# A four-layer graph network on one core: the opening in another order, and x of the fourth layer turned by four transposes and copied across by DMA

## The chip, the cores and the metric

One core of a Trainium2 chip runs the whole program. Its engines are TensorE (PE, with its weight loads shown as PEld), VectorE (DVE), ScalarE (ACT), GpSimd (POOL) and SyncE (SP), which here only issues DMAs. The metric is the device time of one execution in microseconds. The kernel before took 1986.62 us in the median of three runs (1986.0 to 1987.79).

## The reference

x has 16 batches of 1024 nodes with 64 features; `adj` is one 1024 x 1024 integer matrix. Four graph layers follow one another, each as `x = layernorm(x + layer(x, adj))`:

- layers 1 and 3, additive attention: `h = x @ W`, `e = leaky_relu(h@a1 + (h@a2).T)`, masked by `adj`, softmax over the neighbours, `elu(attention @ h)`
- layer 2: a softmax for each feature over the neighbours of `softplus(x*w0 + b0)`
- layer 4, attention by dot products, with the node itself always a neighbour:

```python
h = jnp.einsum('bnc,hdc->bhnd', x, Wh)                 # 4 heads
out_h = _gat_layer(h, mask, bh)                        # softmax(h h^T masked) @ h + b, per head
z = leaky_relu(concat(out_h))
h2 = jnp.einsum('bnk,dk->bnd', z, Wo)
out2 = _gat_layer(h2, mask, bo)                        # the same with one head
```
followed by a leaky ReLU, a layer norm with gamma and beta, the residual and the outer layer norm.

## The kernel before

Nodes lie in 8 tiles of 128 partitions; PSUM banks hold 512 columns. Every engine has its own list of work written out by hand, with semaphores between them; a function of a stage is called from the engine's list at a named place, and the order of the calls is the order on that engine.

**The opening** (`opening`). SP issues eight DMAs of 512 KB, one for each row tile of `adj`, then x of batches 1 to 3, small weights, and x of batches 4 to 15 (3 MB). DVE turns each tile to zeros and ones (L407), PE turns it by eight 128 x 128 transposes into one of two PSUM tiles (L451), and ACT (DVE for the last tile) copies it into `keep.mask` (L434, L420). From the row sums a matrix of empty rows is made and turned by eight matmuls (L470), and DVE writes it to `keep.empty` (L425). Among these stands the preparation of batch 0 of the first layer: x is turned (`turn_x`, four transposes, L783), projected (`project`: L791, L800, L806), and the tops of the scores are found and spread (`find_tile_top`, `turn_top`, `find_minus_top`, `find_top`, `spread_tops`, `copy_tops`); `factors` on ACT makes the rows from which the attention weights come.

**The first layer** (`additive_layers`), batch by batch: DVE makes eight tiles of weights (`weigh`, L609) into a ring of four; PE multiplies each with the values (`multiply`, L846, 16 matmuls); `divide` (L616, L619) ends a batch and stands behind the first `weigh` of the next. At the head of a batch PE projects the next batch (`project(n + 1)`) and multiplies the empty rows (`multiply_empty`, L832).

**The fourth layer** (`dot_layer`). A batch has 20 steps: s0 to s7 for the first pair of heads, r0 to r7 for the second, and e0 to e3 for the second attention of the batch before. In each step PE makes two tiles of scores (for s and r twelve matmuls of 512 columns, L1616, L1619, L1622), does a job that stands at this step if there is one, and multiplies the weights of the step before (L1666, eight matmuls; L1681 in e steps); ACT takes the exponent (L1458), DVE masks (L1212). The jobs that concern x of the next batch: POOL copies x into `x_stage`, each tile twice side by side (L1085, at s0); PE turns it at r3 (`turn_x`, eight transposes, L1527), which gives x turned on partitions 0 to 63 and once more on 64 to 127; ACT rounds it to `x_high` (L1401), DVE makes the rest `x_low` (L1166, at r4); PE makes g from them (`make_g`, at e1, L1537 to L1543), DVE multiplies g with `x_high` (`multiply_g`, L1174, at e1); the scores of the next batch begin at its s0. Both copies of x are wanted by the scores, since two heads are multiplied side by side on the two halves of the partitions; `make_g` wants only the half h of the nodes on half h of the partitions. For batch 0 all this stands in the last batch of the third layer, and for batch 1 at r0 to r4 of batch 0.

SP's list in the fourth layer (`sync`): for each batch `spread_recip(b, 0)` (the sums of pair 0 to DRAM, back, inverted by DVE, out and back broadcast), `swap(b - 1)` (half of h copied to the other half of the partitions, high and low part), `store(b - 2)`, `spread_recip(b, 1)`. SP waits in order at each.

## Time and profile before

| | us |
|---|---|
| three runs | 1986.0, 1986.62, 1987.79 |
| the profiled execution, its own time | 1988.66 |
| its span in the trace | 1986.7 |
| PE busy | 1897.6 (96%) |
| DVE busy | 1634.9 (82%) |
| ACT busy | 1246.8 (63%) |
| POOL busy | 581.4 (29%) |

Busy PE is matmul time with modelled ends; the span is from the first instruction to the last. The mean granted TensorE clock was 0.987 of full speed. The opening and the first batches lie at 0 to 60 us, the fourth layer from about 670 us to the end.

### The profile page before, as it was taken

The numbers are of one execution on the slowest core, as the hardware profiler recorded it, in microseconds if no ns is written. First come the engines' busy times: TensorE is split into PE (matmuls) and PEld (weight loads), VectorE is DVE, ScalarE is ACT, GpSimd is POOL, SyncE is SP. The second block draws the span as 40 slices with busy tenths as digits, with TensorE's granted clock in tenths as the row PEclk, the third lists the DMA queues.
The fourth block names the chain that finished last, engine by engine and source line by source line (L and its number), as shares of the span: only waits on it lengthen the run. The fifth ranks groups of instructions, "written<-read, shape, count | busy, mean of one in ns | idle before, by whom it ended". The sixth has DMA issues, their size and how long they took to land.

```text
span 1986.7 us, 51864 instructions
## 1 busy us (share of the span) xinstructions
PE 1897.6 (96%) x22356; PEld 1178.9 (59%) x22356; DVE 1634.9 (82%) x1944; ACT 1246.8 (63%) x2299; POOL 581.4 (29%) x440
## 2 busy tenths in 40 slices
PE   7999899999999899999999999999999999999995
PEld 5888766777888544554545545555455454554554
DVE  5999868878999777878888788888887888878876
ACT  3777776655777676566565665665656656566562
POOL 0333368762433200113122121231221312212124
PEclk9999999998999999999999999999999999999997
DMA  6000000000000001010110100101001011010011
GB/s 177 3 4 3 3 1 1 1 1 3 3 4 3 2 12 33 13 39 3 37 28 12 39 23 18 28 12 39 28 13 38 6 36 28 12 39 23 18 29 33
DMA packets 51947, 42.19 MB, mean 21 GB/s; under 512 B 35208, under 2 KB 38344, under 8 KB 51720
## 3 DMA queue, kind: packets, MB, share of 16 engines
q1 hardware_dynamic: 49816, 38.46, 7.2%
q8 instruction: 176, 2.88, 0.6%
q10 hardware_dynamic: 1904, 0.43, 0.1%
q14 instruction: 51, 0.42, 0.1%
HBM read 25.76 MB, written 4.72 MB: 15 GB/s over the span
## 4 chain that ended last, share of the span: by engine, by line
PE 60%; DVE 5%; issue 1%; DMA 0%; ACT 0%; SPq 0%; POOL 0%; ACTq 0%; DVEq 0%; POOLq 0%
PE fourth_ps_out L1666 22%; PE fourth_ps_scores L1616 8%; PE fourth_ps_out L1681 6%; PE fourth_ps_scores L1619 5%; PE fourth_ps_scores L1622 5%; DVE fourth_weights L1212 3%; PE fourth_ps_scores L1640 2%; PE fourth_ps_prep L1558 2%; PE fourth_ps_scores L1649 1%; PE fourth_ps_scores L1643 1%; PE fourth_ps_scores L1646 1%; PE fourth_ps_prep L1568 1%; PE fourth_ps_prep L1550 1%; PE fourth_ps_prep L1527 1%; DVE fourth_cat L1191 1%
## 5 line engine op out<-in xcount | busy, mean ns | idle before, releaser
L1212 DVE TENSOR_TENSOR fourth_weights<-fourth_weights,keep_mask 128x1024 f32<-128x1024 f32 x512 | 666.0, 1342 | 109.2 <-ACT fourth_weights L1458 107.2
L1458 ACT ACTIVATE fourth_weights<-fourth_ps_scores 128x1024 f32<-128x1024 f32 x512 | 497.0, 1024 | 347.3 <-PE fourth_ps_scores L1622 326.0
L1666 PE MATMUL fourth_ps_out<-fourth_weights,fourth_x_stage 128*64 128x512 f32 x2048 | 498.2, 605 | 4.9 <-DVE fourth_weights L1212 4.9
L609 DVE SCALAR_TENSOR_TENSOR additive_weights<-additive_ps_row,additive_gain,keep_mask 128x1024 f32<-128x1024 f32 x256 | 319.4, 1267 | 2.7 <-ACT additive_ps_row L724 2.7
L846 PE MATMUL additive_ps_out<-additive_values,additive_weights 128*64 128x65 f32 x8192 | 285.7, 226 | 28.3 <-DVE additive_weights L609 23.5
L846 PEld LDWEIGHTS additive_ps_out<-additive_values,additive_weights 128*64 128x64 f32 x8192 | 258.9, 140 | 53.5 <-DVE additive_weights L609 36.2
L1666 PEld LDWEIGHTS fourth_ps_out<-fourth_weights,fourth_x_stage 128*64 128x64 f32 x2048 | 124.2, 136 | 251.6 <-issue 216.2
L1616 PE MATMUL fourth_ps_scores<-fourth_g_high,fourth_x_high 64*128 64x512 f32 x1024 | 229.5, 445 | 2.1 <-ACT fourth_weights L1458 2.1
L1616 PEld LDWEIGHTS fourth_ps_scores<-fourth_g_high,fourth_x_high 64*128 64x128 f32 x1024 | 95.8, 183 | 200.6 <-issue 102.2
L1619 PE MATMUL fourth_ps_scores<-fourth_g_high,fourth_x_low 64*128 64x512 f32 x1024 | 202.0, 390 | 0.0
L1622 PE MATMUL fourth_ps_scores<-fourth_g_low,fourth_x_high 64*128 64x512 f32 x1024 | 201.6, 389 | 0.0
L1465 ACT ACTIVATE fourth_weights<-fourth_ps_scores 128x1024 f32<-128x1024 f32 x128 | 125.6, 1026 | 113.5 <-PE fourth_ps_scores L1649 109.7
L1219 DVE TENSOR_TENSOR fourth_weights<-fourth_weights,keep_mask 128x1024 f32<-128x1024 f32 x128 | 153.0, 1236 | 41.6 <-ACT fourth_weights L1465 41.6
L1090 POOL TENSOR_TENSOR fourth_biased<-fourth_mixed,keep_rows_in 128x512 f32<-128x512 f32 x15 | 32.0, 2135 | 439.2 <-DVE fourth_mixed L1227 439.2
L1681 PEld LDWEIGHTS fourth_ps_out<-fourth_h_values,fourth_weights 128*64 128x64 f32 x4096 | 124.6, 138 | 29.6 <-issue 29.0
L1681 PE MATMUL fourth_ps_out<-fourth_h_values,fourth_weights 128*64 128x65 f32 x4096 | 133.3, 223 | 0.5 <-DVE fourth_weights L1219 0.5
L1622 PEld LDWEIGHTS fourth_ps_scores<-fourth_g_low,fourth_x_high 64*128 64x128 f32 x1024 | 96.4, 184 | 22.7
L1619 PEld LDWEIGHTS fourth_ps_scores<-fourth_g_high,fourth_x_low 64*128 64x128 f32 x1024 | 96.6, 185 | 11.1
L176 POOL TENSOR_TENSOR additive_norm_rstd<-additive_norm_variances,keep_minus_half 128x8 f32<-128x8 f32 x32 | 53.5, 1670 | 162.2 <-DVE additive_norm_variances L170 162.2
L185 ACT ACTIVATE keep_x<-additive_norm_y,additive_norm_offset,additive_norm_rstd 128x64 f32<-128x64 f32 x256 | 88.0, 429 | 7.4 <-POOL additive_norm_offset L179 7.4
L165 ACT ACTIVATE additive_norm_squares<-additive_norm_y,additive_norm_minus_mean 128x64 f32<-128x64 f32 x256 | 85.2, 340 | 2.5 <-DVE additive_norm_minus_mean L159 2.5
L545 POOL TENSOR_TENSOR additive_values<-additive_hidden,additive_values 128x512 f32<-128x512 f32 x32 | 33.8, 1057 | 155.1 <-ACT additive_values L721 155.1
(243 smaller groups left out, 2762.6 us busy)
## 6 DMA issues: line engine op xcount, KB each, us to landing
fourth_recip_wide<-recip_out SPq DMA_DIRECT2D x128, 128.0 KB, 3.0
opening_adj<-in_adj SPq DMA_DIRECT2D x8, 512.0 KB, 8.2
fourth_h_high<-fourth_h_high SPq DMA_DIRECT2D x32, 128.0 KB, 2.8
fourth_h_low<-fourth_h_low SPq DMA_DIRECT2D x32, 128.0 KB, 2.4
out<-keep_x SPq DMA_DIRECT2D x15, 256.0 KB, 2.6
dens_out<-fourth_mixture SPq DMA_DIRECT2D x64, 4.0 KB
keep_x<-in_x SPq DMA_DIRECT2D x1, 768.0 KB, 13.4
fourth_dens<-dens_out SPq DMA_DIRECT2D x32, 8.0 KB, 1.6
```

Of the source, the lines that this page charges most:

```text
L185: act.activation(x[:, t, :], self.y[n % 2][:, t, :], ACT.Identity, bias=self.offset[:, t:t + 1], scale=self.rstd[:, t:t + 1]).then_inc(x_w ...
L609: dve.scalar_tensor_tensor(out=weights[t % RING][:, :], in0=ps_row[s][:, :], scalar=gain[s][:, t:t + 1], in1=keep.mask[:, t, :].bitcast(F3 ...
L846: last = pe.matmul(ps_out[part, i * WIDE:i * WIDE + AUG], weights[t % RING][:, i * P + c * SIDE:i * P + (c + 1) * SIDE], values[s][:, t, 0 ...
L1212: dve.tensor_tensor(buf, buf, keep.mask[:, st.t, cols(half)].bitcast(F32).unsqueeze(1) .to_broadcast([P, 2, HALF]), ALU.mult).then_inc(wei ...
L1219: dve.tensor_tensor(buf[:, :], buf[:, :], keep.mask[:, 2 * p + u, :].bitcast(F32), ALU.mult)\
L1458: act.activation(weights[st.slot + half][:, :], ps_scores[half][:, :], ACT.Exp)\
L1465: act.activation(weights[slot + u][:, :], ps_scores[u][:, :], ACT.Exp).then_inc(exp_ready, 2)
L1616: pe.matmul(ps_scores[half][:, cols(g)], x_high[s][rows(g), nodes], g_high[pair][rows(g), cols(half)], start=True, stop=False)
L1619: pe.matmul(ps_scores[half][:, cols(g)], x_low[s][rows(g), nodes], g_high[pair][rows(g), cols(half)], start=False, stop=False)
L1622: last = pe.matmul(ps_scores[half][:, cols(g)], x_high[s][rows(g), nodes], g_low[pair][rows(g), cols(half)], start=False, stop=True)
L1666: last = pe.matmul(ps_out[rows(g), cols(half)], x_stage[st.s][:, st.t, g, :], weights[st.slot + half][:, cols(g)], start=(st.t == 0), stop ...
L1681: last = pe.matmul(ps_out[c * SIDE:(c + 1) * SIDE, i * WIDE:i * WIDE + AUG], weights[slot + u][:, i * P + c * SIDE:i * P + (c + 1) * SIDE] ...
```

## The change

Two things are changed.

**The opening's order.** On PE x of batch 0 is turned after mask tile 1 (before: 4), projected after tile 3 (5), its top turned after tile 4 and spread after tile 5 (both after tile 7), x of batch 1 turned after tile 6 (after the tops); batch 1 is projected at the end of the opening's list, ahead of `multiply_empty(0)`, as before, but the call stands in another function. What waited for `empty_ready` (written behind the last read of the PSUM tile that holds the empty rows) in front of batch 1's row matmuls now waits for `last_copied`; the two PSUM tiles `turned0` and `turned1` change places for that, and `first_w` moves to other columns of `ps_x`. On ACT the copies of x, hidden and mean move up among the mask copies; on DVE `copy_w`, `copy_products` and the tops move.

**x of the fourth layer.** `x_stage` holds tile t and tile t + 4 side by side, once each; four transposes then give half h of the nodes on half h of the partitions. ACT and DVE round and lower each half on its 64 partitions. SP copies each half to the other half of the partitions, four DMAs of 128 KB for each batch (`fill_x`); `multiply_g` and the first scores wait for them. In SP's list `fill_x(b + 1)` stands between `swap(b - 1)` and `store(b - 2)`, and those of batches 0 and 1 at its head.

```diff
@@ -339,3 +339,3 @@
     mem.psum("beside1")
-    turned = [mem.psum(f"turned{k}") for k in range(2)]
+    turned = [mem.psum(f"turned{k}") for k in range(2)][::-1]
     degree = mem.sbuf("degree", [P, TILES])
...
@@ -347,3 +347,3 @@
     adj_v = ins["adj"].rearrange("(t p) j -> p t j", p=P)
-    first_w, first_products = additive.ps_x[0:DIM, 0:DIM], additive.ps_row[0][:, 0:P + 1]
+    first_w, first_products = additive.ps_x[0:DIM, HALF:HALF + DIM], additive.ps_row[0][:, 0:P + 1]
 
...
@@ -408,6 +408,10 @@
                               accum_out=degree[:, t:t + 1]).then_inc(masked, 1)
-            if t == 1:
+            if t == 2:
                 weights.copy_w(0, first_w)
-            if t == 3:
+            if t == 4:
                 weights.copy_products(0, first_products)
+            if t == 6:
+                additive.find_tile_top(0)
+        additive.find_minus_top(0)
+        additive.find_top(0)
         dve.wait_ge(masked, TILES)
...
@@ -415,5 +419,3 @@
                           ALU.is_equal).then_inc(empty_ready, 1)
-        additive.find_tile_top(0)
-        additive.find_minus_top(0)
-        additive.find_top(0)
+        additive.copy_tops(0)
         dve.wait_ge(turned_full, TILES)
...
@@ -421,3 +423,2 @@
                         turned[1][:, :].rearrange("j (t i) -> j t i", i=P)).then_inc(last_copied, 1)
-        additive.copy_tops(0)
         dve.wait_ge(consts, 13)
...
@@ -436,8 +437,10 @@
                .then_inc(copied, 1)
-            if i == 4:
+            if i == 1:
                 additive.copy_x(0)
-        additive.copy_hidden(0)
-        additive.copy_mean(0)
+            if i == 3:
+                additive.copy_hidden(0)
+                additive.copy_mean(0)
+            if i == 5:
+                additive.copy_x(1)
         additive.factors(0, 0)
-        additive.copy_x(1)
 
...
@@ -455,13 +458,15 @@
                 weights.turn_w(0, first_w)
+                pe.wait_ge(keep.first_x_loaded, 16)
+                additive.turn_x(0)
             if i == 2:
                 weights.multiply_w(0, first_products)
-            if i == 4:
-                pe.wait_ge(keep.first_x_loaded, 16)
+            if i == 3:
                 pe.wait_ge(weights.prod_ready, 2)
-                additive.turn_x(0)
-            if i == 5:
                 additive.project(0)
-        additive.turn_top(0)
-        additive.spread_tops(0)
-        additive.turn_x(1)
+            if i == 4:
+                additive.turn_top(0)
+            if i == 5:
+                additive.spread_tops(0)
+            if i == 6:
+                additive.turn_x(1)
         pe.wait_ge(copied, TILES - 1)
...
@@ -472,2 +477,3 @@
         last.then_inc(empty_full, 1)
+        additive.project(1)
 
...
@@ -475,3 +481,3 @@
     stage.sync, stage.gpsimd, stage.vector, stage.scalar, stage.tensor = sync, gpsimd, vector, scalar, tensor
-    stage.empty_ready = empty_ready
+    stage.empty_ready, stage.last_copied = empty_ready, last_copied
     return stage
...
@@ -857,3 +863,4 @@
             ahead = b + 1 < BATCH
-            if ahead:
+            if ahead and n:
+
                 project(n + 1)
...
@@ -918,3 +925,3 @@
     h_norm = sb("h_norm", [P, HALF], F32R)
-    x_stage = [sb(f"x_stage{k}", [P, TILES, 2, DIM]) for k in range(2)]
+    x_stage = [sb(f"x_stage{k}", [P, PER_BANK, HALVES, DIM]) for k in range(2)]
     x_high = [sb(f"x_high{k}", [P, NODES], F32R) for k in range(2)]
...
@@ -1028,2 +1036,10 @@
 
+    def fill_x(b, s):
+
+        for parts, ready, filled in ((x_high[s], x_high_ready, x_high_filled), (x_low[s], x_low_ready, x_low_filled)):
+            sp.wait_ge(ready, 2 * (b + 1))
+            for h in range(HALVES):
+                sp.dma_start(parts[rows(1 - h), cols(h)].bitcast(F32), parts[rows(h), cols(h)].bitcast(F32))\
+                  .then_inc(filled, 16)
+
     def spread_recip(b, pair):
...
@@ -1063,2 +1079,4 @@
     def sync():
+        fill_x(0, 0)
+        fill_x(1, 1)
         for b in range(BATCH):
...
@@ -1067,2 +1085,4 @@
                 swap(b - 1)
+            if b and b + 1 < BATCH:
+                fill_x(b + 1, 1 - b % 2)
             if b > 1:
...
@@ -1084,4 +1104,5 @@
         wait(pool, weights_used, used)
-        pool.tensor_copy(x_stage[s][:, :, :, 1:DIM], keep.x[:, b, :, 1:DIM].unsqueeze(2)
-                         .to_broadcast([P, TILES, 2, DIM - 1])).then_inc(staged, 1)
+
+        pool.tensor_copy(x_stage[s][:, :, :, 1:DIM],
+                         keep.x[:, b, :, 1:DIM].rearrange("p (h t) d -> p t h d", h=HALVES)).then_inc(staged, 1)
 
...
@@ -1163,6 +1184,6 @@
     def lower_x(b, s):
+        dve.wait_ge(x_high_ready, 2 * b + 2)
         for h in range(HALVES):
-            dve.wait_ge(x_high_ready, 2 * b + h + 1)
-            dve.tensor_tensor(x_low[s][:, cols(h)], ps_prep[:, cols(h)], x_high[s][:, cols(h)].bitcast(F32),
-                              ALU.subtract).then_inc(x_low_ready, 1)
+            dve.tensor_tensor(x_low[s][rows(h), cols(h)], ps_prep[rows(h), cols(0)],
+                              x_high[s][rows(h), cols(h)].bitcast(F32), ALU.subtract).then_inc(x_low_ready, 1)
 
...
@@ -1172,2 +1193,3 @@
         dve.wait_ge(g_full, n + 1)
+        dve.wait_ge(x_high_filled, 32 * (b + 1))
         wait(dve, norm_full, n)
...
@@ -1398,5 +1420,5 @@
     def round_x(b, s):
+        act.wait_ge(x_full, b + 1)
         for h in range(HALVES):
-            act.wait_ge(x_full, 2 * b + h + 1)
-            act.activation(x_high[s][:, cols(h)], ps_prep[:, cols(h)], ACT.Copy).then_inc(x_high_ready, 1)
+            act.activation(x_high[s][rows(h), cols(h)], ps_prep[rows(h), cols(0)], ACT.Copy).then_inc(x_high_ready, 1)
 
...
@@ -1525,7 +1547,6 @@
         pe.wait_ge(staged, b + 1)
-        for t in range(TILES):
-            last = pe.transpose(ps_prep[:, chunk(t)], x_stage[s][:, t, :, :].rearrange("p k c -> p (k c)"),
+        for t in range(PER_BANK):
+            last = pe.transpose(ps_prep[:, chunk(t)], x_stage[s][:, t, :, :].rearrange("p h c -> p (h c)"),
                                 keep.ident[:, :])
-            if t % PER_BANK == PER_BANK - 1:
-                last.then_inc(x_full, 1)
+        last.then_inc(x_full, 1)
 
...
@@ -1611,2 +1632,4 @@
             pe.wait_ge(x_low_ready, 2 * (st.b + 1))
+            pe.wait_ge(x_high_filled, 32 * (st.b + 1))
+            pe.wait_ge(x_low_filled, 32 * (st.b + 1))
         pair, s, nodes = st.phase, st.s, chunk(st.t)
...
@@ -1665,3 +1688,3 @@
             for g in range(2):
-                last = pe.matmul(ps_out[rows(g), cols(half)], x_stage[st.s][:, st.t, g, :],
+                last = pe.matmul(ps_out[rows(g), cols(half)], x_stage[st.s][:, st.t % PER_BANK, st.t // PER_BANK, :],
                                  weights[st.slot + half][:, cols(g)], start=(st.t == 0),
...
@@ -2520,3 +2543,3 @@
             if n == 1:
-                nc.tensor.wait_ge(start.empty_ready, 2)
+                nc.tensor.wait_ge(start.last_copied, 1)
             if n == BATCH:
```

PE in the opening, kernel before, from the transposes of mask tile 3 to the turning of batch 1's x (`turned` are the PSUM tiles of the mask and of the empty rows, `ps_x` and `ps_row` hold the projections):

```order
L451 MATMUL opening_turned1<-keep_ident,opening_rows 128x128 x8
L451 MATMUL opening_turned0<-keep_ident,opening_rows 128x128 x8
L783 MATMUL additive_ps_x<-keep_ident,keep_x 128x128 x4
L451 MATMUL opening_turned1<-keep_ident,opening_rows 128x128 x8
L791 MATMUL additive_ps_x<-keep_w_aug0,additive_x_sum0 128x64
L800 MATMUL additive_ps_x<-keep_w_aug0,additive_x_turned 128x65 x8
L806 MATMUL additive_ps_row0<-additive_x_turned,keep_w_wide0 128x512 x2
L451 MATMUL opening_turned0<-keep_ident,opening_rows 128x128 x8
L451 MATMUL opening_turned1<-keep_ident,opening_rows 128x128 x8
L813 MATMUL additive_ps_x<-keep_ident,additive_tile_top 1x128
L818 MATMUL additive_ps_x<-additive_top_pair,keep_ones 128x2
L783 MATMUL additive_ps_x<-keep_ident,keep_x 128x128 x4
```

The same place now, from mask tile 3 to the empty rows:

```order
L454 MATMUL opening_turned0<-keep_ident,opening_rows 128x128 x8
L797 MATMUL additive_ps_x<-keep_w_aug0,additive_x_sum0 128x64
L806 MATMUL additive_ps_x<-keep_w_aug0,additive_x_turned 128x65 x8
L812 MATMUL additive_ps_row0<-additive_x_turned,keep_w_wide0 128x512 x2
L454 MATMUL opening_turned1<-keep_ident,opening_rows 128x128 x8
L819 MATMUL additive_ps_x<-keep_ident,additive_tile_top 1x128
L454 MATMUL opening_turned0<-keep_ident,opening_rows 128x128 x8
L824 MATMUL additive_ps_x<-additive_top_pair,keep_ones 128x2
L454 MATMUL opening_turned1<-keep_ident,opening_rows 128x128 x8
L789 MATMUL additive_ps_x<-keep_ident,keep_x 128x128 x4
L454 MATMUL opening_turned0<-keep_ident,opening_rows 128x128 x8
L475 MATMUL opening_turned1<-keep_ident,opening_empty_wide 128x128 x8
```

The turning of x has gone up past tiles 2 to 4 and stands above this piece; the projection has gone up past tiles 4 and 5, the tops and batch 1's x past tile 7, so that only the empty rows stand behind tile 7. The projection of batch 1 follows them in both kernels.

DVE in the opening, kernel before, from mask tile 4 to the first attention weights (L407 masks a tile, L414 writes the empty rows, L420 copies the last mask tile):

```order
L407 TENSOR_SCALAR opening_rows,opening_degree<-opening_adj 128x1024 x4
L414 TENSOR_SCALAR opening_empty_wide<-opening_degree 128x1024
L586 TENSOR_REDUCE additive_tile_top<-additive_hidden 128x1
L591 TENSOR_REDUCE additive_top_pair<-additive_ps_x 1x1
L596 TENSOR_SCALAR additive_top_pair<-additive_top_pair 1x1
L420 CAST keep_mask<-opening_turned1 128x8x128
L601 COPY additive_tops<-additive_ps_x 128x2
L425 TENSOR_SCALAR keep_empty<-opening_turned0,opening_row_used 128x1024
L609 SCALAR_TENSOR_TENSOR additive_weights0<-additive_ps_row0,additive_gain0,keep_mask 128x1024
```

The same place now, from mask tiles 5 and 6:

```order
L407 TENSOR_SCALAR opening_rows,opening_degree<-opening_adj 128x1024 x2
L592 TENSOR_REDUCE additive_tile_top<-additive_hidden 128x1
L407 TENSOR_SCALAR opening_rows,opening_degree<-opening_adj 128x1024
L597 TENSOR_REDUCE additive_top_pair<-additive_ps_x 1x1
L602 TENSOR_SCALAR additive_top_pair<-additive_top_pair 1x1
L418 TENSOR_SCALAR opening_empty_wide<-opening_degree 128x1024
L607 COPY additive_tops<-additive_ps_x 128x2
L422 CAST keep_mask<-opening_turned0 128x8x128
L426 TENSOR_SCALAR keep_empty<-opening_turned1,opening_row_used 128x1024
L615 SCALAR_TENSOR_TENSOR additive_weights0<-additive_ps_row0,additive_gain0,keep_mask 128x1024
```

The top of the tiles (`tile_top`), which waits for ACT's copy of the projection, now stands in front of the last mask tile, and the other tops in front of the empty rows and the last mask copy.

SP in the fourth layer, kernel before, batch 2's part (`x_high1` and `x_low1` are the buffers of batch 3):

```order
L1034 DMA dens_out<-fourth_mixture0 1x1024 x2
L1037 DMA fourth_dens<-dens_out 128x16
L1040 DMA recip_out<-fourth_head_recip 128x16
L1046 DMA fourth_recip_wide0<-recip_out 64x512 x4
L1022 DMA fourth_h_high<-fourth_h_high 64x512 x2
L1026 DMA fourth_h_low<-fourth_h_low 64x512 x2
L1052 DMA out<-keep_x 128x8x64
L1034 DMA dens_out<-fourth_mixture1 1x1024 x2
```

The same place now:

```order
L1050 DMA dens_out<-fourth_mixture0 1x1024 x2
L1053 DMA fourth_dens<-dens_out 128x16
L1056 DMA recip_out<-fourth_head_recip 128x16
L1062 DMA fourth_recip_wide0<-recip_out 64x512 x4
L1030 DMA fourth_h_high<-fourth_h_high 64x512 x2
L1034 DMA fourth_h_low<-fourth_h_low 64x512 x2
L1042 DMA fourth_x_high1<-fourth_x_high1 64x512 x2
L1042 DMA fourth_x_low1<-fourth_x_low1 64x512 x2
L1068 DMA out<-keep_x 128x8x64
L1050 DMA dens_out<-fourth_mixture1 1x1024 x2
```

Two rows of two DMAs each are new, in front of the store and of the sums of pair 1.

## Rows read from the trace of the kernel before

**Rows 1.** The page, section 4: the chain that ended last, by engine.

```profile
PE 60%; DVE 5%; issue 1%; DMA 0%; ACT 0%; SPq 0%; POOL 0%; ACTq 0%; DVEq 0%; POOLq 0%
```

**Rows 2.** Windows: stretch, its length; busy PE, PEld, DVE, ACT, POOL; clock, DMA.

```profile
1236.76:1317.44 80.68, 80.33 (x697) 42.19 (x695) 67.14 (x65) 49.28 (x58) 19.02 (x11) 1.00 0.09 25
```

**Rows 3.** Timeline of PE, fourth layer: start, us, instruction (steps r2, r3).

```profile
1255.90 0.66 PE L1599 MATMUL fourth_ps_prep<-keep_ident,fourth_h_plain 128*128 128x128 f32 x4
...
1259.95 1.09 PE L1527 MATMUL fourth_ps_prep<-keep_ident,fourth_x_stage 128*128 128x128 f32 x8
```

**Rows 4.** Timeline of PE, step s2; then waits of 860 to 1900 us.

```profile
1225.58 1.08 PE L1666 MATMUL fourth_ps_out<-fourth_weights,fourth_x_stage 128*64 128x512 f32 x4 [0.35 <-DVE fourth_weights L1212]
...
PE fourth_ps_out L1666 <- DVE fourth_weights L1212: 4.3, 12, 0.4
```

**Rows 5.** Timelines of POOL and DVE there; L1085 by source; DVE in batch 15.

```profile
1222.37 2.07 POOL L1085 COPY fourth_x_stage<-keep_x 128x1008 f32<-128x1008 f32 x1
...
1223.47 2.05 DVE L1212 TENSOR_TENSOR fourth_weights<-fourth_weights,keep_mask 128x1024 f32<-128x1024 f32 x1
...
L1085 POOL COPY fourth_x_stage<-keep_x x16: 1021/2072/2073, 649.3 to 1787.2; 128x1008 f32<-128x1008 f32 x16
...
1867.91 4.69 DVE L1212 TENSOR_TENSOR fourth_weights<-fourth_weights,keep_mask 128x1024 f32<-128x1024 f32 x4
```

**Rows 6.** SP's issues, their landing (L1022), and DVE, steps r4 to e1.

```profile
1268.24 1.24 SPq L1026 DMA_DIRECT2D fourth_h_low<-fourth_h_low  x2
...
DMA to landing us min/median/max: 2.5/2.8/3.8
...
1284.46 1.22 DVE L1174 TENSOR_TENSOR fourth_products<-fourth_ps_prep,fourth_x_high 128x1024 fp32r<-128x1024 f32 x1 [2.07 <-PE fourth_ps_prep L1543]
```

**Rows 7.** Timelines of ACT and DVE, batch 0 of the fourth layer.

```profile
704.96 1.08 ACT L1401 ACTIVATE fourth_x_high<-fourth_ps_prep 128x512 fp32r<-128x512 f32 x2
...
710.23 1.23 DVE L1174 TENSOR_TENSOR fourth_products<-fourth_ps_prep,fourth_x_high 128x1024 fp32r<-128x1024 f32 x1 [0.80 <-PE fourth_ps_prep L1543]
```

**Rows 8.** Timeline of PE in the opening.

```profile
5.99 1.94 PE L451 MATMUL opening_turned<-keep_ident,opening_rows 128*128 128x128 f32 x8 [5.99 <-DVE opening_rows L407]
...
10.56 0.31 PE L210 MATMUL additive_ps_x<-keep_ident,keep_w 64*64 64x64 f32 x1 [0.28 <-DMA keep_a_cols<-in_L_gnn_a]
...
14.45 0.80 PE L224 MATMUL additive_ps_row<-weights_a_wide,weights_w_turned 64*128 64x129 f32 x2
...
18.79 1.04 PE L451 MATMUL opening_turned<-keep_ident,opening_rows 128*128 128x128 f32 x8
...
20.20 0.43 PE L791 MATMUL additive_ps_x<-keep_w_aug,additive_x_sum 128*128 128x64 f32 x2 [0.38 <-ACT additive_x_turned L688]
20.57 1.11 PE L800 MATMUL additive_ps_x<-keep_w_aug,additive_x_turned 64*128 64x65 f32 x16
21.51 1.08 PE L806 MATMUL additive_ps_row<-additive_x_turned,keep_w_wide 64*128 64x512 f32 x4
...
25.43 0.38 PE L813 MATMUL additive_ps_x<-keep_ident,additive_tile_top 128*1 128x128 f32 x2 [0.94 <-DVE additive_tile_top L586]
...
27.16 1.95 PE L470 MATMUL opening_turned<-keep_ident,opening_empty_wide 128*128 128x128 f32 x16
```

**Rows 9.** Timeline of DVE, opening to the end of batch 0.

```profile
29.23 1.28 DVE L425 TENSOR_SCALAR keep_empty<-opening_turned,opening_row_used 128x1024 fp32r<-128x1024 f32 x1 [1.73 <-PE opening_turned L470]
...
30.43 2.47 DVE L609 SCALAR_TENSOR_TENSOR additive_weights<-additive_ps_row,additive_gain,keep_mask 128x1024 f32<-128x1024 f32 x2
...
46.46 0.21 DVE L616 RECIPROCAL additive_recip<-additive_ps_out 128x8 f32<-128x8 f32 x1 [1.82 <-PE additive_ps_out L846]
```

**Rows 10.** Timeline of PE in batch 0; window 33 to 34 us.

```profile
35.15 1.15 PE L846 MATMUL additive_ps_out<-additive_values,additive_weights 128*64 128x65 f32 x32
...
43.52 1.15 PE L846 MATMUL additive_ps_out<-additive_values,additive_weights 128*64 128x65 f32 x32 [1.66 <-issue]
...
33.00:34.00 1.00, 1.00 (x4) 0.00 (x0) 0.98 (x2) 0.10 (x1) 0.00 (x0) 0.50 1.04 215
```

5 lines of the change are left out of this document (3 added, 2 removed).

## The prediction

> **What bounds the kernel now.** I read the page first, then the fourth layer batch by batch, then the opening. The chain that ended last is on PE for 60% of the span and hardly anywhere else [rows 1]; the reader is to see that what leaves PE's own list is worth its full time as long as nothing else takes its place. The window over one batch of the fourth layer shows how far that holds: PE is busy for 80.33 of 80.68 us, DVE for 67.1, ACT for 49.3 [rows 2]. Only 0.35 us of a batch are idle on PE, and the timeline names them: one wait at step s2, for DVE's masked weights; 12 of them in the stretch of 860 to 1900 us, 4.3 us together [rows 4]. The opening is another matter: there PE, ACT and DVE wait for each other, the first attention weights of batch 0 start at 30.43 us, and batch 0 ends, by the division, at 46.46 [rows 9]. From there on the first layer runs at its own pace, so what that division gains is the gain of the whole opening.
>
> **The change part by part.** *Four transposes fewer on PE.* Eight transposes of staged x take 1.09 us, four transposes of the same shape (h, one step earlier) 0.66 [rows 3]. Both rows carry the same tail of the last matmul, so four fewer save 0.43 us. PE has no gap around them, so this is on the path, 15 times in the fourth layer (batches 1 to 15): 6.5 us. For batch 0 they stand in the third layer's last batch, where ACT waits for them; I count 0.43 there too. Sum 6.9, bounds 6.0 and 7.0.
>
> *POOL's copy halved.* The copy of 1008 elements took 1.02 us at its shortest and 2.07 in the median [rows 5]. At s1 it starts at 1222.37, at the same moment as a mask multiplication of DVE, and ends at 1224.44; the next multiplication of DVE, begun at 1223.47, takes 2.05 us, where an undisturbed one takes half of 2.36 or so: in batch 15, which has no copy, four take 4.69 us, 1.17 each [rows 5]. So the two take turns, and DVE pays some 0.85 us for the copy. Those are the weights for which PE waits 0.35 us at 1225.58 [rows 4], and the wait is missing in batch 15. With 504 elements the copy's own turn is half, 0.5 us, and DVE is free about 0.5 us earlier: more than 0.35, so the wait should go, with 0.15 to spare. 13 batches (2 to 14) have both copy and wait: 13 x 0.35 = 4.6 us. Bounds: 0, if DVE is held as long as before or the stall is only shifted, and 4.9.
>
> The Trainium skill's page "SBUF — State Buffer", section "Who interferes with whom", gives the mechanism: a DVE instruction with two SBUF inputs and a GpSimd instruction that reads SBUF exclude each other for the whole instruction, whichever comes first. By that rule the hold is the copy's own length, and the trace agrees (2.05 against 1.17 us).
>
> *ACT and DVE on 64 partitions.* Two roundings and two subtractions of 512 columns remain, each on half the partitions. Two roundings take 1.08 us [rows 7], over 512 columns each; nothing here shows half the partitions to be faster, and neither engine is on the path at r3 or r4. I take nothing; bounds 0 and 0.
>
> *Four DMAs for each batch.* SP issues two transfers of 128 KB in 1.24 us, and such a transfer lands 2.5 to 3.8 us after its issue [rows 6]. In SP's list the new ones come after the swap of h, whose last pair is issued at 1268.24 to 1269.48. So they are issued until about 1272, and land by 1275.5. The first reader, `multiply_g` on DVE, starts at 1284.46 [rows 6], 9 us later, and behind it stand the masks of step e1, for which PE would wait. The store and the sums of pair 1 behind them in SP's queue come later than 1272 anyway. Cost 0, and the cover is 9 us. The tight place is batch 0, where x of batch 1 is rounded until 706.04 and multiplied at 710.23 [rows 7]: two issues of 0.6 us and a landing of 2.8 make 709.6, by the slowest landing 710.5. That is 0 to 0.3 us, once. Transfers on disjoint halves of the partitions are advised against in the skill ("DMA: Bandwidth & Descriptors", "Rules for kernel authors": they serialize); even four after each other, 4 x 2.8 = 11 us from 1269.5, end before 1284.46 here.
>
> *The opening, first part: when the first weights can start.* The last things ahead of them are tile 7, the empty rows on PE and their copy on DVE. PE's new list is now nearly without gaps, so I add it up from the weights' arrival at 10.56 [rows 8]: turning W 0.31, x 0.66 [rows 3], tile 2 1.94, the products 0.80, tile 3 1.94; this makes 16.2. Then the projection 0.43 + 1.11 + 1.08 and four tiles of 1.04 (the fast rate, which before was reached by 18.79), two small matmuls for the tops of 0.38, x of batch 1 0.66: 24.4. The empty rows 1.95, and DVE's copy 1.28 [rows 9]: 27.6, against 30.43. ACT's copies run beside it, the last one perhaps 0.2 late: 27.8. Gain 2.6; bounds 1.5 and 4. (That DVE now waits for the projection before the last tile costs nothing as long as PE is the later one.)
>
> *The opening, second part: batch 0.* Before, DVE had its weights ready from 31.7, but PE multiplied the first only at 35.15 [rows 10], since the projection of batch 1 waited for x, turned late. In that stretch PE's granted clock was 0.50, i.e. 1.2 instead of 2.4 GHz, after half-idle microseconds (33 to 34 in rows 10). Now x of batch 1 is ready during the opening; its projection follows the empty rows at 26.4 and is over by 29, when the first weights come. Batch 0 then goes at DVE's pace: nine multiplications of 1.2 (two take 2.47, rows 9) and 0.7 of small ones, 11.5 us to the division, where before it took 46.46 - 30.43 = 16.0. So the division could stand at 27.8 + 11.5 = 39.3, 7.2 us earlier. One piece of the old delay I keep: at 41.9 PE stopped for 1.66 us, for nothing that the profile shows, in the middle of one tile's products [rows 10], while the 3 MB of x were still landing. Those come at the same time as before, and PE now runs more instructions beside them. With 1.7 off I take 5.5 for the whole opening; bounds 2.6 (all of the second part is eaten up) and 7.5.
>
> The skill ("Runtime: NRT & Kernel Launch", "Instruction fetch mechanics") says that instructions stream in by blocks over the engine's own DMA queue, mostly hidden. The gap of 1.66 us is not hidden; if it is the fetch, by that page's claim it would be an exception, and without it the opening would gain 7.2.
>
> **The sum.** 5.5 + 6.9 + 4.6 = 17.0 us. Against the profiled execution's own 1988.66 (span 1986.7) this gives 1971.7; that execution is 2.0 above the median of 1986.62, so the median after is 1969.6.
>
> **The rivals.** (1) *The wait at s2 stays.* For it: the copy has a four-deep access pattern now and POOL's spans are rough; 0.15 us to spare is little. Against: batch 15. It gives 1986.6 - 12.4 = 1974.2. (2) *The opening gains only its first part.* For it: the unexplained 1.66 us under the load; the division can't come before PE has finished, and each stop like that counts nearly in full. Against: DVE, not PE, sets the pace afterwards. 2.6 + 6.9 + 4.6 = 14.1: 1972.5. Both together 1977.1. (3) *All of it and the gap too*: 7.2 + 6.9 + 4.6: 1967.9. (4) *Slower.* One mechanism: `multiply_g` waits in each batch for the two high copies, and holds the masks behind it. The two are issued at 1269.5 and 1270.1 and cost nothing until one lands later than 1284.46, some 14 us after its issue, against 3.8 at most seen [rows 6]; to end at slower by 0.2% (4 us) it must eat the 17 as well, 21 us over 14 batches, 1.5 us each, a landing of 16 us. It would give 1990.6. Only SP arriving late at `fill_x` could do it, if the sums of pair 0 ran that late; they don't [rows 6]. (5) *The change doesn't do what it says*: PE's saved time turns up as waiting for ACT's exponents. Against it, ACT is idle for 31 us of a batch and DVE for 13 [rows 2]. It would leave the opening and the wait: 1976.5.
>
> **How the numbers follow.** Forecast (every term near its middle) 52%; rival 1 14%; rival 2 14%, both together 4%; rival 3 9%; rival 5 4%; slower 2%; about no change 1%. The range from 1966 to 1976.5 takes in the first five but the doubled one and half of rival 5. A measurement of this kernel can tell 0.2%, 4 us, from no change. Faster by over 0.2%: 97%; within: 1%; slower: 2%.
>
> **What would show it.** In the changed kernel's trace: the division of batch 0 near 41 us; the first weights near 27.8 and the first products by 30; four transposes of staged x in a 0.66 row; no wait of PE at s2 and the mask multiplication beside the copy near 1.6 us; the period of a batch 80.68 - 0.78 = 79.9 us; the new copies issued near r4 and landing before e0. A period of 80.25 would mean that the wait has stayed, one of 80.68 that the transposes were covered, one above that new waits came in. The forecast is wrong if the period is off by more than 0.3 us or the division of batch 0 stands outside 39 to 44 us.

## The result and the profile after

The changed kernel takes 1972.62 us in the median of four runs (1971.68 to 1975.19), beside 1987.18 us for the kernel before on the same chip: a ratio of 0.9929, 95% interval 0.9918 to 0.9941. The gain is 14.6 us; 17.0 were forecast, and the time is 3.0 us over the predicted 1969.6, inside the range. The kernel before was timed anew beside every run below, with medians from 1987.18 to 1988.95 us, so ratios compare two runs better than their medians do.

The profiled execution had a time of its own of 1975.19 us and a span of 1973.1, 13.6 us less than the 1986.7 of before. Three marks cut both spans into stages: the division of batch 0 (the opening's end), and the first and the last product over x in the fourth layer. All marks are starts of instructions. The profiled execution is the slowest of the four, 2.6 us above their median.

| stage | before | after | gain | forecast |
|---|---|---|---|---|
| start to the division of batch 0 | 46.46 | 42.68 | 3.8 | 5.5 |
| from there to the first product over x | 627.5 | 626.3 | 1.1 | 0.43 |
| first to last product over x (s, r, e steps) | 1251.1 | 1239.2 | 11.9 | 11.05 |
| last product over x to the end | 61.7 | 64.9 | -3.2 | 0 |

So the two middle rows came out a little better than forecast, the first gained less, and the last stage became longer, which no term of the sum had.

*Opening.* Timeline of DVE in the changed kernel (start, duration, instruction, in brackets the idle time before it), answering to [rows 9]:

```profile
25.37 1.28 DVE L426 TENSOR_SCALAR keep_empty<-opening_turned,opening_row_used 128x1024 fp32r<-128x1024 f32 x1 [1.73 <-PE opening_turned L475]
26.57 2.47 DVE L615 SCALAR_TENSOR_TENSOR additive_weights<-additive_ps_row,additive_gain,keep_mask 128x1024 f32<-128x1024 f32 x2
...
42.68 0.21 DVE L622 RECIPROCAL additive_recip<-additive_ps_out 128x8 f32<-128x8 f32 x1 [4.80 <-PE additive_ps_out L852]
```

The first weights start at 26.57, against 30.43 before and 27.8 in the forecast. The division waits 4.80 us for PE. The timeline of PE says why, beside [rows 8, 10], and the windows below it (stretch, length, busy PE, PEld, DVE, ACT, POOL with counts, granted clock, DMA share, GB/s) show what came with it:

```profile
14.02 1.24 PE L454 MATMUL opening_turned<-keep_ident,opening_rows 128*128 128x128 f32 x8
...
27.99 1.15 PE L852 MATMUL additive_ps_out<-additive_values,additive_weights 128*64 128x65 f32 x32
...
32.53 2.25 PE L852 MATMUL additive_ps_out<-additive_values,additive_weights 128*64 128x65 f32 x69
38.17 4.48 PE L852 MATMUL additive_ps_out<-additive_values,additive_weights 128*64 128x65 f32 x91 [3.38 <-issue]
```

```profile
36.00:38.00 2.00, 0.00 (x0) 0.00 (x0) 1.88 (x2) 0.00 (x0) 0.00 (x0) 1.00 1.08 221
38.00:40.00 2.00, 1.83 (x34) 1.83 (x36) 0.00 (x0) 0.00 (x0) 0.00 (x0) 0.56 1.12 219
40.00:42.00 2.00, 2.00 (x48) 2.00 (x46) 0.00 (x0) 0.00 (x0) 0.00 (x0) 0.58 0.94 187
```

The reader is to see three things. The projection of batch 1 and the first products came as planned, by 30. Then PE stopped for 3.38 us behind its 165th product, the same place where it had stopped for 1.66 us before. And after the stop the granted clock was 0.56 to 0.58, close to the lower of its two levels (0.50, 1.2 GHz), so that the last 91 products took 4.48 us. Before, at a granted clock of 1.00, they took 2.90:

```profile
43.52 2.90 PE L846 MATMUL additive_ps_out<-additive_values,additive_weights 128*64 128x65 f32 x91 [1.66 <-issue]
```

From the first weights to the division it was 16.0 us before (30.43 to 46.46) and 16.1 after (26.57 to 42.68). So the whole gain of the opening, 3.8 us, lies ahead of the first weights, and the second part of the forecast (11.5 us for this stretch, and 1.7 for the stop) brought nothing.

*Fourth layer.* One batch, by windows [rows 2]; the four transposes [rows 3]; POOL's copy and DVE's multiplications beside it [rows 5]; SP's issues [rows 6]:

```profile
1206.59:1286.44 79.85, 79.85 (x697) 41.69 (x689) 66.94 (x64) 49.39 (x58) 18.58 (x11) 1.00 0.13 33
...
1249.49 0.66 PE L1549 MATMUL fourth_ps_prep<-keep_ident,fourth_x_stage 128*128 128x128 f32 x4
...
1212.37 1.65 POOL L1106 COPY fourth_x_stage<-keep_x 128x504 f32<-128x504 f32 x1
...
1212.34 5.03 DVE L1234 TENSOR_TENSOR fourth_weights<-fourth_weights,keep_mask 128x1024 f32<-128x1024 f32 x4
...
1257.80 1.24 SPq L1034 DMA_DIRECT2D fourth_h_low<-fourth_h_low  x2
1259.08 1.24 SPq L1042 DMA_DIRECT2D fourth_x_high<-fourth_x_high  x2
1260.36 1.24 SPq L1042 DMA_DIRECT2D fourth_x_low<-fourth_x_low  x2
...
1273.61 1.23 DVE L1196 TENSOR_TENSOR fourth_products<-fourth_ps_prep,fourth_x_high 128x1024 fp32r<-128x1024 f32 x1 [2.10 <-PE fourth_ps_prep L1564]
```

PE is busy for the whole 79.85 us; the period was forecast as 79.9. The wait of [rows 4] is gone in every batch but the first. The four multiplications beside the copy take 5.03 us, where four with no copy took 4.69 [rows 5]; the one that the copy holds takes 1.63 us, as forecast (near 1.6), instead of 2.05. `multiply_g` (L1196) starts 13.3 us after both high DMAs were issued and waits for PE, not for a DMA.

*The end.* PE's waits in each kernel, the changed one first (engine, what it waits to write, for whom; us in total, times, longest):

```profile
PE fourth_ps_scores L1610 <- DVE fourth_cat L1267: 4.5, 1, 4.5
```

```profile
PE fourth_ps_scores L1589 <- DVE fourth_cat L1245: 2.7, 1, 2.7
```

DVE in turn waited there for the reciprocals of the last heads, sent to memory and spread from there; after, then before:

```profile
1926.62 0.69 DVE L1264 TENSOR_TENSOR fourth_cat<-fourth_ps_prep,fourth_sloped 128x512 f32<-128x512 f32 x1 [2.70 <-DMA fourth_recip_wide<-recip_out]
```

```profile
1941.70 0.69 DVE L1242 TENSOR_TENSOR fourth_cat<-fourth_ps_prep,fourth_sloped 128x512 f32<-128x512 f32 x1 [0.95 <-DMA fourth_recip_wide<-recip_out]
```

The DMA views of the 4 us around that small write of 8 KB (issued at 1917.74 after, 1934.56 before) show a packet of the queue q8, which carries PE's instructions, in one and none in the other. After:

```profile
q1 hardware_dynamic: 144, 0.01, 2.3%
q8 instruction: 1, 0.02, 1.6%
...
recip_out<-fourth_head_recip SPq DMA_DIRECT2D x1, 8.0 KB, 3.1
```

Before:

```profile
q1 hardware_dynamic: 280, 0.24, 21.9%
...
recip_out<-fourth_head_recip SPq DMA_DIRECT2D x1, 8.0 KB, 1.4
```

(The larger count of q1 before is the spreading of the reciprocals, which begins sooner behind the early landing.) After, the write lands after 3.1 us instead of 1.4. Narrower windows show what held it. The write is 128 packets of 64 bytes and 16 of 4 bytes, 144 in all. Changed kernel, 1918.4 to 1919.2 us, then 1919.6 to 1920.0; nothing moves between them:

```profile
q1 hardware_dynamic: 135, 0.01, 10.9%
q8 instruction: 1, 0.02, 8.0%
...
q1 hardware_dynamic: 9, 0.00, 1.5%
```

The packet of instructions starts 0.93 us after the write's issue and takes 1.02; the last 9 packets of the write (one sixteenth of 144, so probably the share of one of the 16 DMA engines) move only when it is over, at 2.0 us. Before, all 144 had moved in the microsecond from 1935 to 1936. The late landing made 1.7 us; PE then waited 4.5 us, its clock fell (0.50 from 1930 to 1934 us; the second half of the output projection took 1.97 us instead of 1.08), and 3.2 us were lost in all.

### The profile page after: what moved, and what is told of

It reads as the page before. It is cut to its first block, busy times and chain, and to the rows that moved or that the text cites. A ratio compares the mean times of both kernels' runs of the same rounds, so it can differ in the third digit from the quotient of the medians.

```text
span 1973.1 us, 51833 instructions
## 1 busy us (share of the span) xinstructions
PE 1888.3 (96%) x22292; PEld 1169.6 (59%) x22292; DVE 1632.1 (83%) x1944; ACT 1248.5 (63%) x2299; POOL 574.9 (29%) x440
## 4 chain that ended last, share of the span: by engine, by line
PE 64%; DVE 1%; DMA 0%; ACT 0%; issue 0%; POOL 0%; SPq 0%; ACTq 0%; DVEq 0%; POOLq 0%
PE fourth_ps_out L1689 24%; PE fourth_ps_scores L1639 9%; PE fourth_ps_out L1704 6%; PE fourth_ps_scores L1642 6%; PE fourth_ps_scores L1645 6%; PE fourth_ps_scores L1663 2%; PE fourth_ps_prep L1579 2%; PE fourth_ps_scores L1666 2%; PE fourth_ps_scores L1672 1%; PE fourth_ps_scores L1669 1%; PE fourth_ps_prep L1589 1%; PE fourth_ps_prep L1571 1%; PE fourth_ps_prep L1620 0%; PE fourth_ps_prep L1549 0%; PE fourth_ps_prep L1564 0%; PE fourth_ps_prep L1561 0%
## 5 line engine op out<-in xcount | busy, mean ns | idle before, releaser
L852 PE MATMUL additive_ps_out<-additive_values,additive_weights 128*64 128x65 f32 x8192 | 286.3, 227 | 30.9 <-DVE additive_weights L615 24.3
L852 PEld LDWEIGHTS additive_ps_out<-additive_values,additive_weights 128*64 128x64 f32 x8192 | 259.6, 140 | 56.0 <-DVE additive_weights L615 37.2
L1642 PEld LDWEIGHTS fourth_ps_scores<-fourth_g_high,fourth_x_low 64*128 64x128 f32 x1024 | 96.5, 185 | 11.2
```

Of the source, the lines that this page charges most:

```text
L852: last = pe.matmul(ps_out[part, i * WIDE:i * WIDE + AUG], weights[t % RING][:, i * P + c * SIDE:i * P + (c + 1) * SIDE], values[s][:, t, 0 ...
L1642: pe.matmul(ps_scores[half][:, cols(g)], x_low[s][rows(g), nodes], g_high[pair][rows(g), cols(half)], start=False, stop=False)
```

## The experiments

Two theories for the stop of PE in batch 0. **Load theory:** PE's own instructions come in blocks through the DMA engines, and a block is late while the 3 MB of x fill them. **Place theory:** the stop belongs to its place in PE's list. For the rest: each term of the sum by itself.

### The halves of the change: open_only, turn_only

`open_only` has the changed code up to the first layers and the fourth layer of before; `turn_only` the reverse.

> The opening's new order alone; x is turned by eight transposes as before. If the two halves of the change are independent: first weights of batch 0 near 26.6 us, division of batch 0 at 42.7 as in the changed kernel (PE stopped for about 3.4 us in batch 0), period of a fourth-layer batch 80.7 with the wait at s2, total about 4 to 5 us under the kernel before: 1982.5. Rival: the opening's gain is eaten up by the second layer, then within 1 us of the kernel before.

> The turning of x alone (four transposes, halved copy on POOL, DMAs for the rest); the opening is the old one. Forecast from the prediction's terms: 6.9 + 4.6 = 11.5 us under the kernel before, 1975.7; period 79.86; division of batch 0 at 46.5 with the stop of 1.7 us. With open_only the two gains should add up to the whole (14.6 measured); a sum over 17 would mean that the parts disturb each other.

Measured: open_only 1982.92 us, ratio 0.9973 [0.9963, 0.9983]; turn_only 1978.07, 0.9950 [0.9935, 0.9965]; the kernel before beside them 1987.85. The gains are 4.9 and 9.8, 14.7 together, beside 14.6 for the whole: they add up, as far as intervals of 2 to 3 us to either side can tell. turn_only stays 1.7 short of its forecast; its trace has the full 12.0 between the first and the last product over x, and the late write at the end as well (3.6 us to landing, 64.1 us from the last product to the end).

### The load: load_late, load_parts, load_split, before_parts

```
# load_late: one line ahead of the 3 MB load
+ sp.wait_ge(additive.mixed_ready, 2)
# load_parts (and before_parts, the same on the kernel before)
- sp.dma_start(keep.x[:, 4:BATCH, :, :], x_rows(ins)[:, 4:BATCH, :, :]).then_inc(keep.x_loaded[1], 16)
+ for b in range(4, BATCH):
+     sp.wait_ge(additive.mixed_ready, 2 * (b - 3))
+     if b > 4:
+         sp.wait_ge(keep.x_loaded[1], 16 * (b - 4))
+     sp.dma_start(keep.x[:, b, :, :], x_rows(ins)[:, b, :, :]).then_inc(keep.x_loaded[1], 16)
# load_split: the loop with its dma_start alone, no waits
# in load_parts, before_parts and load_split PE's waits for x_loaded[1] count the twelve loads
```

> The changed kernel, with the 3 MB of x (batches 4 to 15) issued only after batch 0 has been divided. Theory (PE's own instruction stream waits behind the load): no stop of PE in batch 0, the division near 39 us instead of 42.7, but a stop of 1 to 4 us in batch 1 or 2, between 40 and 60 us, while the load runs then; total 1970 to 1973. Rival (the stop belongs to the place in PE's list): the stop of about 3.4 us stays at the 165th product of batch 0, division at 42.7, total 1972.6.

> The changed kernel, with the 3 MB of x in twelve loads of 256 KB, one after each division of batches 0 to 11. Theory (instructions wait behind the load): stops of at most about 1 us, division of batch 0 near 39 us, what follows 4 us earlier, total near 1968.6. Rival (the place in the list): the stop stays, 1972.6. Rival (each small load stops PE for about 1 us): twelve small stops, total above 1975.

> The changed kernel with the 3 MB of x cut into twelve loads of 256 KB as in load_parts, but issued one behind the other at the old place, with no pause between them. Theory (a block of instructions waits as long as the queues of the DMA engines are full, whatever the loads' size): the stop in batch 0 stays, 3 us or so, total 1972.6. Rival (a single large load is the trouble): stop under 1 us, division of batch 0 near 38 us, total near 1968.

> The kernel before, with x loaded in twelve pieces, one after each division, and nothing else changed. Theory (the stop of 1.66 us at the 165th product is the load's doing): no stop, division of batch 0 at about 44.8 instead of 46.5, total 1.7 us less, 1985.5. Rival (the place in the list): stop and time unchanged, 1987.2. It also gives what the opening's order is worth where no load stands in its way: division here against load_parts' 37.8 us, about 7.

Measured: load_late 1976.82, 0.9943 [0.9928, 0.9958]; load_parts 1967.83, 0.9901 [0.9885, 0.9918]; load_split 1965.38, 0.9884 [0.9869, 0.9898]; before_parts 1985.54, 0.9987 [0.9977, 0.9997].

In load_late the stop moved with the load. Timeline of PE, batch 1, and the window there:

```profile
51.80 1.03 PE L853 MATMUL additive_ps_out<-additive_values,additive_weights 128*64 128x65 f32 x27 [2.73 <-issue]
```

```profile
50.00:60.00 10.00, 8.20 (x114) 6.31 (x115) 3.52 (x6) 2.10 (x6) 1.86 (x2) 0.66 0.41 86
```

Batch 0 was divided at 36.67 there, 6 us earlier than in the changed kernel, but the third division stands at 69.27 against 69.17: all was given back. The place theory has fallen. The total of 1976.82 is above the expected 1970 to 1973. It is 4.2 over the changed kernel's by the medians, 2.8 by the ratios, whose intervals overlap, and 1.3 by the spans of the two traces; the rest stays open.

The traces also tie each stop to a block of instructions. In all nine profiles with a stop, PE goes on 2.7 to 2.9 us after a packet of q8 has started: 35.41 and 38.17 in the changed kernel, 40.84 and 43.52 before, 39.87 and 42.62 in turn_only, 49.05 and 51.80 in load_late. And the place is a fixed one in PE's list. Counted with weight loads and semaphore instructions, 705 instructions lie ahead of the stop in all eight profiles that stop in batch 0. In load_late it is 1473, which is 768 more, exactly three blocks of 256.

In load_parts and load_split there is no stop, and the divisions stand at 37.82 and 37.10. In load_parts 256 KB moved once in each batch; its total is within 0.8 us of the expected 1968.6. load_split was a miss of the load theory as I had put it: the queues were not empty, and I had expected the stop. What differs is how long a block of instructions waits. The DMA views of 26 to 34 us, first of the changed kernel, then of load_split, by queue (packets, MB, share of 16 engines):

```profile
q1 hardware_dynamic: 1445, 1.45, 85.2%
...
keep_x<-in_x SPq DMA_DIRECT2D x1, 0.2 KB, 17.6
```

```profile
q1 hardware_dynamic: 6543, 1.65, 110.3%
q8 instruction: 1, 0.02, 1.0%
...
keep_x<-in_x SPq DMA_DIRECT2D x8, 256.0 KB, 4.9
```

With the single load no block of instructions moved in these 8 us; the next came at 35.4, and PE went on at 38.17. In load_parts, where no load runs then, it came at 30.2. In load_split, whose twelve issues take SP 14.04 us, it came at 30.9, although the engines were as busy as in the changed kernel (1.65 MB in these 8 us against 1.45). So the cause is that the load is one DMA, and not the bytes that move. What it is about the one DMA, no run separates. Two things differ: all of it is handed over at once and lands 17.6 us after the issue, a small load after 4.9; and its packets are of 1 KB (1445 packets for 1.45 MB), those of the small loads of 256 bytes (6543 for 1.65 MB). The twelve are also handed over no faster than they move: an issue takes SP 1.17 us there, and 0.37 in load_parts. A single load with packets of 256 bytes was not run. Where the block waits, the traces don't show either. The Trainium skill ("Runtime: NRT & Kernel Launch", "Instruction fetch mechanics") says that instructions are fetched in blocks of 16 KiB, 256 instructions, mostly hidden. The changed kernel's page agrees on the block: section 3 has, for PE's 22,292 matmuls and as many weight loads,

```profile
q8 instruction: 176, 2.88, 0.6%
```

which is 253 instructions to a packet of 16 KB, and 256 with PE's 549 semaphore instructions. But the crossing was not hidden at this place: it cost 1.66 us before and 3.38 after.

before_parts gives the fourth corner. Division of batch 0, means over the profiled executions (in brackets how many, and the lowest and highest):

| | one load of 3 MB at the old place | load later, or in twelve pieces |
|---|---|---|
| old order of the opening | 46.0 (2: 45.56, 46.46) | 43.59 (1) |
| new order | 42.1 (6: 41.15 to 42.86) | 37.2 (5: 36.63 to 37.89) |

The last cell holds load_late, load_parts, combined, load_split and split_sooner. The new order is worth 3.9 us under the load and 6.4 without it; the load costs the old order 2.4 us and the new one 4.9. The first weights themselves start anywhere from 25.13 to 26.75 us with the new order, so the stretch from them to the division tells more: 11.4 us in each of these five, beside the 11.5 of the sum, and 16.1 in the changed kernel; in the old order 14.3 without the load and 16.0 under it. before_parts had no stop and gained 1.9 us, as expected (1.7), but its division came 1.2 us before the expected 44.8.

### The wait at s2 and the transposes: long_copy, turned_twice

```
# long_copy: the stage holds everything twice, the second set is not read
- x_stage = [sb(f"x_stage{k}", [P, PER_BANK, HALVES, DIM]) for k in range(2)]
+ x_stage = [sb(f"x_stage{k}", [P, 2, PER_BANK, HALVES, DIM]) for k in range(2)]
...
+     .unsqueeze(1).to_broadcast([P, 2, PER_BANK, HALVES, DIM - 1])).then_inc(staged, 1)
# turned_twice
- for t in range(PER_BANK):
+ for t in [*range(PER_BANK)] * 2:
```

> The changed kernel with POOL's copy of staged x made as long as before (1008 elements, each value written twice; the second set is not read), four transposes and the DMAs kept. Theory (DVE is held for the length of the copy): the mask multiplication beside it takes about 2.05 us again, PE waits 0.35 us at s2 in 13 batches, period 80.25 instead of 79.86, total 4.6 us over the changed kernel, 1977.2. Rival (the wait went because the copy's pattern or the list around it changed): period 79.86, 1972.6.

> The changed kernel with its four transposes of staged x done twice over, into the same place (eight in all). Theory (each four are on the path with 0.43 us): period 79.86 + 0.43 = 80.29 with no wait at s2; 6.9 us in all over the changed kernel, 1979.5. It also adds 128 instructions to PE's list (64 matmuls and their weight loads), half a block of its instruction stream at the end: if it is such a block that delayed the last reciprocals, they may land early here (1.4 us after their issue instead of 3.1), and the end is 2 to 3 us shorter: 1977. Rival (the transposes are covered by waiting for DVE): period 79.86, 1972.6.

Measured: long_copy 1978.61, 0.9955 [0.9941, 0.9970]; turned_twice 1979.20, 0.9952 [0.9936, 0.9969]. Timelines of POOL, DVE and PE in long_copy, then its waits:

```profile
1213.27 2.07 POOL L1106 COPY fourth_x_stage<-keep_x 128x1008 f32<-128x1008 f32 x1
...
1213.23 5.46 DVE L1235 TENSOR_TENSOR fourth_weights<-fourth_weights,keep_mask 128x1024 f32<-128x1024 f32 x4
...
1216.47 1.08 PE L1690 MATMUL fourth_ps_out<-fourth_weights,fourth_x_stage 128*64 128x512 f32 x4 [0.35 <-DVE fourth_weights L1235]
...
PE fourth_ps_out L1690 <- DVE fourth_weights L1235: 4.8, 14, 0.4
```

The longer copy alone brings the wait back, in the same place and size; the period is 80.25 (1213.27 to 1293.52), and the stretch between first and last product over x grows from 1239.2 to 1244.5, 5.3 us. In turned_twice the period is 80.23 and that stretch 1245.1: four transposes more cost 5.9 us in 14 or 15 batches, about 0.41 each. The two together explain 11.2 of the 11.9 us; the other 0.7 stay open. In the medians both came out slower than expected: long_copy by 1.4 us (1977.2), turned_twice by 2.2 (1977 with an early landing at the end).

turned_twice tested the end as well, and there the expectation held: its write of the last reciprocals landed in 1.4 us. With the half block of added instructions, the packet of q8 nearest to the write starts 1.7 us before its issue and is over before any of the write moves:

```profile
recip_out<-fourth_head_recip SPq DMA_DIRECT2D x1, 8.0 KB, 1.4
```

From the last product over x to the end it took 62.1 us. In the profiles that keep the last inversion at e2 this stretch goes with that one landing: where SP waited 1.42 or 1.43 us for it (before, open_only, before_parts, turned_twice, load_split) it is 60.6 to 62.1 us long; where SP waited 3.1 to 3.6 us (the changed kernel, turn_only, load_late, long_copy, fills_twice) 63.6 to 65.1, and in each of these five a packet of instructions moves in the stretch of the landing. load_parts lies between, with 2.5 and 61.9 us. The length of PE's list alone doesn't decide it: load_split has the changed kernel's list, and its packet starts 1.66 us after the issue, when the write has landed. Tenths of a microsecond do: in turn_only the packet starts at 1.60 us, and yet 9 packets of the write come behind it, at 2.5. Why they hadn't moved with the other 135, at 0.75 to 1.1 us, stays open.

### The DMAs: fills_twice

```
+ wait(sp, again_filled, 64 * b)
+ for parts, again in ((x_high[s], again_high), (x_low[s], again_low)):
+     for h in range(HALVES):
+         sp.dma_start(again[rows(1 - h), :], parts[rows(h), cols(h)].bitcast(F32)).then_inc(again_filled, 16)
```

> The changed kernel with each batch's four fills of x issued a second time, behind the first four, into memory that nobody reads; SP issues eight DMAs of 128 KB where there were four. Theory (a cover of 9 us and more, nothing waits for SP here): period 79.86, total within 1 us of the changed kernel, 1972.6. Rival (SP's queue is nearly on the path: the store and the sums of pair 1 stand behind them): period above 80.5, total above 1982.

Measured: 1973.35, 0.9925 [0.9910, 0.9940], beside the changed kernel's 0.9929. The period is 79.83. The DMAs cost nothing, nor would twice as many. In the changed kernel they are issued 0.6 us apart and land 2.2 to 3.7 us after their issues, so the 11 us that the prediction allowed for them one after the other were not needed.

### The end, and a better kernel: recip_sooner, combined, split_sooner

```
- if at == "e2":
+ if at == ("e1" if st.last else "e2"):
      invert_heads(b, 1)
```

> The changed kernel; in the last batch alone, DVE inverts the sums of heads 2 and 3 one step sooner (before the masks of e2 instead of behind them). Theory (at the end of the x heads the program waits for the reciprocals' way through memory, 1.0 us where no block of instructions is in its way and 2.7 to 3.3 where one is): no wait of DVE for the spread reciprocals, PE's wait ahead of the second output projection under 2 us instead of 4.5, PE's clock does not fall there; total 1 to 3 us under the changed kernel, near 1970.5. Rival (that wait was hidden by others): no change, 1972.6.

> The changed kernel with both: x in twelve loads and the last reciprocals one step sooner. Expected: the gain of load_parts (4.8) and that of recip_sooner, which has little left over where the reciprocals came early anyway: 1966.5, between 1965.5 and 1968. Rival: the shorter program puts a wait elsewhere at the end, 1968 or more.

> load_split and recip_sooner together: x in twelve loads one behind the other, and the last reciprocals one step sooner. Expected: no stop in batch 0, the division near 37 us, no wait of DVE for the spread reciprocals whatever block of instructions comes by, so the end after the last product over x of 60.5 to 62 us. Since load_split's own last reciprocals came early (1.4 us after their issue), little is left: 1964.5 to 1966, against load_split's 1965.4. Rival (load_split's gain was one lucky place of the blocks of instructions): the stop or the late reciprocals come back, 1968 or more.

Measured: recip_sooner 1971.86, 0.9920 [0.9904, 0.9936]; combined (with load_parts) 1966.89, 0.9895 [0.9879, 0.9912]; split_sooner (with load_split) 1967.67, 0.9895 [0.9878, 0.9911]. The mechanism works in the trace, if not in full (PE still waits 2.5 us, where under 2 were expected): in recip_sooner DVE waits for ACT, no more for the DMA,

```profile
1925.06 0.69 DVE L1264 TENSOR_TENSOR fourth_cat<-fourth_ps_prep,fourth_sloped 128x512 f32<-128x512 f32 x1 [0.70 <-ACT fourth_sloped L1528]
...
PE fourth_ps_scores L1610 <- DVE fourth_cat L1267: 2.5, 1, 2.5
```

and the end takes 61.9 us instead of 64.9 (61.5 and 61.4 in the other two). But in the times it is not told apart: 0.8 us under the changed kernel, with overlapping intervals. A loss of 3 us at the end may thus belong to the profiled execution and not to every one; the others have no trace. Where the write landed early anyway it brings nothing, as split_sooner shows beside load_split: it was expected at 1964.5 to 1966 and came 1.7 us above that, close to its rival's 1968. combined met its 1966.5. The best median of all is load_split, 1965.38, 7 us under the changed kernel (9 by the ratios) and with an interval clear of it; load_parts, combined and split_sooner have intervals that overlap with it.

## Why the prediction was right, and where it was off

The forecast held: faster, 1972.62 in a range of 1966 to 1976.5. The fourth layer came by the mechanism that was named. The opening's figure came in part by luck, since two errors of opposite sign lie in it, and the total lies on rival 2's 1972.5 only because a loss at the end, which was in no sum, met small gains elsewhere. By its steps:

- *Four transposes fewer*, 6.9: right. The row of 0.66 stands there, and four more cost 5.9 (turned_twice; the term has 6.45 for that stretch). Rival 5 (the time turns up as waiting) is refuted: PE is busy for all 79.85 us of a batch.
- *POOL's copy halved*, 4.6: right in cause and size. The wait is gone, and the longer copy alone brings it back (long_copy, 5.3 us). Rival 1 (the wait stays) is refuted. The Trainium skill's page "SBUF — State Buffer", section "Who interferes with whom", by which the hold would be the copy's own length, is borne out in the difference: DVE's four multiplications take 0.43 us more (5.46 against 5.03) when the copy is 0.42 us longer (2.07 against 1.65). Half the elements are not half the copy, though: at its shortest it took 1.02 us with 1008 elements and 0.60 with 504, where the forecast had 0.5. So the multiplication beside it became 0.42 us shorter (2.05 to 1.63), of which 0.35 were needed.
- *64 partitions and four DMAs*, 0: right (fills_twice); rival 4 had nothing to start from. The tight place of batch 0 is mis-added in the prediction: 706.04, two issues of 0.6 and a landing of 2.8 make 710.0, not 709.6. It didn't matter, for no `multiply_g` waits for a DMA, in batch 0 neither.
- *The opening, first part*, 2.6: too low, it gained 3.9. PE's rows were at the fast rate sooner than in [rows 8]: tile 3 took 1.24 us at 14.02, where I had added 1.94. The sum also adds the projection's three rows at full length, 2.6 us, but they overlap: the next row starts 2.2 us after the first of them. PE then waited 0.82 us for ACT's copy of the mask, more than the 0.2 that were allowed.
- *The opening, second part*: the step that failed is "One piece of the old delay I keep". The term of 1.66 us was mis-sized. Without the single load the division stands at 37.2, earlier than the 39.3 of the sum only because the first weights are; the 11.5 us behind them are right (11.4). Under the load it stands at 42.1, since the old 1.66 became a stop of 3.2 to 3.4 us plus 1.6 us or more for the lower clock after it: 4.7 us from the first weights on, where the sum had 1.7. (The row 33 to 34 of [rows 10], which the prediction calls half idle, has PE busy throughout; it shows the clock of 0.50, the idle time lies before it.) PE comes to its 165th product 7 us sooner, in the middle of the load instead of at its end, while the block of instructions is held back by 5 us in either place (35.4 instead of 30.2 us; in the old order 40.8 instead of the 35.7 of before_parts). The whole opening gained 3.8 in the pair of profiles, 3.9 by the means, for 5.5. Rival 2 named this mechanism, and it is what happened: the opening gained its first part alone. Only that part was larger than its 2.6. The sign for the forecast being wrong, a division outside 39 to 44 us, was too wide to show this.
- *The end*, not in the sum: 3.2 us lost in the profiled execution. Nothing that the change does is near it. The list of PE became shorter by 96 instructions, so the places where its blocks are fetched moved, and one of them fell on a small DMA that others wait for. I had asked of every added DMA what it collides with, and not of PE's instructions.

In the sum: 17.0 forecast, less 1.7 in the opening and 3.2 at the end, plus 0.9 in the fourth layer and 0.7 between, the last without a known cause, make the 13.6 of the spans.

## What to carry to other kernels

A gap of PE that "waits for nothing" during a large load is worth an experiment before any work on the order around it: here twelve loads for one (load_split) brought 7 us, half of what the whole change had brought. To see whether it is the instruction stream, look for a packet of the instruction queue shortly before the engine goes on. When work is moved earlier, ask what it moves into; a stop that lay at the end of a load may come to lie in its middle, and cost PE's clock as well. And after a change of PE's instruction count, look at each short DMA on the critical path again, even far from the change.

## What the runs showed of the hardware that was not expected

- Under one DMA of 3 MB the block of PE's instructions moved at 35.4 us instead of 30.2, 5 us later; under twelve of 256 KB, moving as many bytes in the stretch, at 30.9. PE went on 2.7 to 2.9 us after the packet's start in all nine profiles with a stop.
- A block of instructions (16 KB) beside an 8 KB write of 144 packets went with a landing of 3.1 to 3.6 us instead of 1.4: in the changed kernel 135 packets moved at once and the last 9 only behind the block.
- After a stop of 3.38 us PE was granted 0.56 to 0.58 of its clock from 38 to 42 us; after one of 1.66 us (before) or 0.94 (turn_only) it stayed at 1.00.
